# Products that nobody reads in four places, the first expert splits on ScalarE, one weight load and two read-outs moved

## What is computed

```python
x = L0_attn_resid_pre                                   # (2, 512, 256)
x = x + _L0_attn_ref(_layernorm(x), ...)   # 16 heads of 128, rotary, causal;
                                           # weights sgn*exp(|s| - max|s|), normed by their sum
x = x + _L0_ffn_ref(_layernorm(x), ...)    # routed in groups, top 4 of 16 experts
x = x + _L1_attn_ref(_layernorm(x), ...)   # 16 heads of 16, rotary, plain softmax
x = x + _L1_ffn_ref(_layernorm(x), ...)    # top 4 of 16 experts
# one expert: silu(x @ g.T) * (x @ u.T) @ d.T, times the token's weight, summed; a shared one without weight
```

## Time and profile before

| what | value |
|---|---|
| time, median of 3 runs | 890.24 us (885.75 to 897.82) |
| the profiled execution | 885.39 us, of which the span 883.7 us |
| PE, share of the span | 93% |
| DVE, ACT, POOL | 75%, 59%, 53% |
| mean granted TensorE clock | 0.984 |

### The profile page before, as it was taken

One profiled execution on the slowest core, in us unless ns is written; L12 is line 12 of the kernel. 1 busy time (PEld: TensorE's weight loads), 2 busy tenths in 40 slices (PEclk: granted clock), 3 DMA queues, 4 the chain that ended last, 5 costly groups with the idle time before them and its releaser, 6 DMA issues.

```text
span 883.7 us, 14685 instructions
## 1 busy us (share of the span) xinstructions
PE 825.5 (93%) x4500; PEld 625.8 (71%) x4500; DVE 659.3 (75%) x1354; ACT 519.3 (59%) x1099; POOL 468.9 (53%) x400
## 2 busy tenths in 40 slices
PE   4899999999999999878998999999999988999997
PEld 3678888778688888656787888654444446888886
DVE  5799999999988999788376865866777643576554
ACT  3688888778788888562544533354566564454442
POOL 3556666666456565533666776531300524566774
PEclk9999999999999999999999999978999999999999
DMA  4223222222332222112665458312431123334441
GB/s 141 104 96 97 96 95 95 96 96 86 127 96 96 95 95 96 48 67 73 206 221 180 137 156 281 116 57 75 130 132 50 55 74 114 117 122 139 149 155 66
DMA packets 57857, 99.97 MB, mean 113 GB/s; under 512 B 8320, under 2 KB 19072, under 8 KB 57792
## 3 DMA queue, kind: packets, MB, share of 16 engines
q1 hardware_dynamic: 57792, 99.17, 33.9%
HBM read 72.67 MB, written 9.57 MB: 93 GB/s over the span
## 4 chain that ended last, share of the span: by engine, by line
PE 64%; issue 12%; DVE 12%; POOL 9%; ACT 3%; DMA 1%; DVEq 0%; POOLq 0%; ACTq 0%; SPq 0%
PE ps L917 9%; PE ps L894 9%; PE ps L903 8%; PE ps L319 6%; PE ps L382 4%; PE ps L330 4%; PE ps L370 3%; POOL q_sin L515 3%; PE ps L1585 3%; PE ps L1555 3%; PE ps L343 3%; PE ps L1468 3%; PE ps L357 2%; PE ps L1489 2%; DVE nm L1779 2%
## 5 line engine op out<-in xcount | busy, mean ns | idle before, releaser
L1044 POOL TENSOR_TENSOR ew_lo<-ew_raw,ew_hi 128x768 fp32r<-128x768 f32 x68 | 127.7, 1879 | 69.3 <-ACT ew_hi L1009 41.3
L991 ACT ACTIVATE hid_hi<-guw 128x512 fp32r<-128x512 f32 x68 | 43.0, 632 | 160.2 <-POOL guw L1060 108.0
L1060 POOL TENSOR_TENSOR guw<-gu,cwb 128x512 f32<-128x512 f32 x64 | 84.7, 1324 | 98.2 <-issue 73.8
L1099 DVE TENSOR_TENSOR hid_lo<-guw,hid_hi 128x512 fp32r<-128x512 f32 x68 | 78.7, 1158 | 76.1 <-ACT hid_hi L991 76.0
L1779 DVE TENSOR_REDUCE nm<-ps 128x1 f32<-128x512 f32 x128 | 81.3, 684 | 24.7 <-PE ps L1489 24.5
L1674 ACT ACTIVATE e<-ps 128x512 f32<-128x512 f32 x128 | 69.0, 598 | 38.4 <-PE ps L1585 38.0
L502 DVE SCALAR_TENSOR_TENSOR w<-ex,rden,sgn 128x512 f32<-128x512 f32 (+3 forms) x128 | 90.9, 772 | 0.0
L430 ACT ACTIVATE ex<-sabs,nmax 128x512 f32<-128x512 f32 (+3 forms) x128 | 61.5, 552 | 43.1 <-DVE nmax L476 43.1
L515 POOL TENSOR_TENSOR q_sin<-q_sw,sin 128x512 f32<-128x512 f32 x64 | 85.0, 1348 | 1.4 <-DMA q_sw<-q_in 1.2
L917 PE MATMUL ps<-ew_hi,hid_hi 128*128 128x256 f32 x272 | 78.6, 289 | 5.9 <-DVE hid_lo L1099 4.4
L917 PE MATMUL ps<-ew_lo,hid_hi 128*128 128x256 f32 x272 | 77.2, 284 | 0.0
(11 more groups left out here) (181 smaller groups left out, 2403.9 us busy)
## 6 DMA issues: line engine op xcount, KB each, us to landing
ew_raw<-in_ew SPq DMA_DIRECT2D x68, 384.0 KB, 3.2
q_sw<-q_in SPq DMA_DIRECT2D x128, 128.0 KB, 2.0
cwb<-cw_dram SPq DMA_DIRECT2D x64, 256.0 KB, 3.7
wqk_raw<-in_wqk SPq DMA_DIRECT2D x32, 256.0 KB, 2.6
wv_raw<-in_wv SPq DMA_DIRECT2D x32, 128.0 KB, 2.6
wo_raw<-in_wo SPq DMA_DIRECT2D x32, 128.0 KB, 2.1
qs<-stk_q SPq DMA_DIRECT2D x16, 256.0 KB, 3.5
ks<-stk_k SPq DMA_DIRECT2D x16, 256.0 KB, 4.1
```

The source lines that it names most:

```text
L1044: pool.tensor_tensor(ff[f].ew[1][:, i % EW_SLOTS, :], ew_raw[:, i % RAW_SLOTS, :], fp(ff[f].ew[0][:, i % EW_SLOTS, :]), ALU.subtract).then ...
L1060: pool.tensor_tensor(ff[f].guw[:, i % 2, :], ff[f].gu[:, i % 2, :], ff[f].cwb[:, r % CWB_SLOTS, :], ALU.mult).then_inc(sem("guw"), 1)
L1099: dve.tensor_tensor(ff[f].hid[1][:, i % 2, :], ff[f].guw[:, i % 2, :], fp(ff[f].hid[0][:, i % 2, :]), ALU.subtract).then_inc(sem("hid_lo"), 1)
```

## The change

`warm` issues products on PE whose result no one reads: the bank that they write is overwritten by the next product there. It stands in four places: 14 at the start, as soon as the memset of `ones_r` on DVE is done, 10 more when the first `rstd` is made, 7 after the transposes of the output biases in step -2, and 2 ahead of each of the score tiles 26 to 31. The high parts of the expert items 0 to 4 are made on ACT at the end of the steps 27 to 31, ahead of what ACT did there; DVE made them in the steps 28 to 32. POOL's part of the norm and of the routing weights moves from step 27 to step 28. The load of item 8 moves behind the loads of the fourth and fifth `cwb` in both layers. In layer 1 the read-out of the last quad moves ahead of the activation of row 5, and its `normal` on DVE from row 6 to row 5.

```diff
@@ -613,7 +613,7 @@
                 pool.wait_ge(sem("xn"), NT)
                 pool.tensor_tensor(x[:, t:t + 2, :], x[:, t:t + 2, :],
                                    bo_row[:, 0, :].unsqueeze(1).broadcast_to([P, 2, D]), ALU.add).then_inc(sem("x_bo0"), 1)
-            if i == N0 - 5:
+            if i == N0 - 4:
                 ln_pool(pool, 1, (0,))
                 gw_low(pool, 0)
             if N0 - 4 <= i <= N0 - 1:
@@ -626,6 +626,11 @@
                 ew_low(pool, 0, 5)
                 weighted(pool, 0, 3)
 
+        def warm(pe, count, bank, src):
+
+            for _ in range(count):
+                pe.matmul(ps[:, bank, :], src[:, 0:P], src[:, 0:S], start=True, stop=True)
+
         def bias_rows(pe, k):
             for h in range(8 * k, 8 * k + 8):
                 last = pe.transpose(ps[:, BV_BANK[k] + h % 8 // 4, h % 4 * P:(h % 4 + 1) * P],
@@ -646,6 +651,7 @@
                         last = pe.transpose(ps[:, 7, k * D + c * P:k * D + (c + 1) * P],
                                             bo_in[:, k, c:c + 1].broadcast_to([P, P]), ident[:, :])
                 last.then_inc(sem("bo_ps"), 1)
+                warm(pe, 7, 3, ones_r)
             if i == N0 - 3:
                 pe.wait_ge(sem("q_rot"), 2 * N0)
                 ln_pe(pe, 1, (0,))
@@ -670,6 +676,8 @@
                 bias_rows(pe, 1)
 
         def a0_at_act(act, i):
+            if N0 - 5 <= i < N0:
+                ew_high_act(act, 0, i - (N0 - 5))
             if i == -3:
                 ln_act(act, 0, (0,))
                 act.wait_ge(sem("tab0"), 80)
@@ -710,22 +718,16 @@
                 ln_stats(dve, 1, 0)
             if i == N0 - 4:
                 ln_xn(dve, 1, 0)
-                ew_high_dve(dve, 0)
             if i == N0 - 3:
                 ln_low(dve, 1, 0)
-                ew_high_dve(dve, 1)
             if i == N0 - 2:
-                ew_high_dve(dve, 2)
                 gated(dve, 0, 0)
                 hid_low(dve, 0, 0)
                 routes[0] = ffn_route(dve, 0)
                 for part in range(3):
                     next(routes[0])
             if i == N0 - 1:
-                ew_high_dve(dve, 3)
                 next(routes[0])
-            if i == N0:
-                ew_high_dve(dve, 4)
             if i in (H0, N0):
                 h = i // H0 - 1
                 dve.wait_ge(sem("x_bo0"), 2 * h + 2)
@@ -755,7 +757,6 @@
         LAG3 = 9
         LOOP_AT = 4
         SPLIT_AHEAD = 2
-        FIRST_SPLITS = 5
         CWB_SLOTS = 3
         GU_BANKS = ((5, 6), (4, 7))
         GU_LATE = (2, 3)
@@ -836,7 +837,7 @@
             cw_store(0)
             for r in range(CWB_SLOTS):
                 cwb_load(r)
-            for i in range(2 * RAW_SLOTS, 3 * RAW_SLOTS):
+            for i in range(2 * RAW_SLOTS, 3 * RAW_SLOTS - 1):
                 ew_load(sp, f, i)
             for i, (m, h) in enumerate(ITEMS):
                 if i == CW1_AT[f]:
@@ -847,7 +848,7 @@
                     cwb_load(ROUTED[i] + 1)
                 if f == 0:
                     a1_row_sp(sp, i)
-                if LOOP_AT <= i and i + SPLIT_AHEAD + RAW_SLOTS < NI:
+                if LOOP_AT <= i + 1 and i + SPLIT_AHEAD + RAW_SLOTS < NI:
                     ew_load(sp, f, i + SPLIT_AHEAD + RAW_SLOTS)
 
         def logits(pe, f, h):
@@ -1000,15 +1001,13 @@
             wait_f(eng, f, f"ew_ld{i % RAW_SLOTS}", 16 * (i // RAW_SLOTS + 1))
             wait_f(eng, f, "y", i + 1 - EW_SLOTS)
 
-        def ew_high_dve(dve, i):
-            ew_high(dve, 0, i)
-            dve.tensor_copy(ff[0].ew[0][:, i % EW_SLOTS, :], ew_raw[:, i % RAW_SLOTS, :]).then_inc(sem("ew_hi_dve"), 1)
-
         def ew_high_act(act, f, i):
             ew_high(act, f, i)
             act.activation(ff[f].ew[0][:, i % EW_SLOTS, :], ew_raw[:, i % RAW_SLOTS, :], ACT.Copy).then_inc(sem("ew_hi_act"), 1)
 
         def row_act(act, f, i):
+            if (f, i) == (1, TAIL_ZT):
+                read_out(act, QUADS - 1)
             if i > LAG3:
                 hid_high(act, f, i - 1)
             silu_of(act, f, i)
@@ -1037,10 +1036,7 @@
                 a1_row_act(act, NI)
 
         def ew_low(pool, f, i):
-            if f == 0 and i < FIRST_SPLITS:
-                pool.wait_ge(sem("ew_hi_dve"), i + 1)
-            else:
-                pool.wait_ge(sem("ew_hi_act"), f * NI + i + 1 - FIRST_SPLITS)
+            pool.wait_ge(sem("ew_hi_act"), f * NI + i + 1)
             pool.tensor_tensor(ff[f].ew[1][:, i % EW_SLOTS, :], ew_raw[:, i % RAW_SLOTS, :], fp(ff[f].ew[0][:, i % EW_SLOTS, :]),
                                ALU.subtract).then_inc(sem("ew_lo"), 1)
 
@@ -1251,6 +1247,7 @@
         STEPS = QUADS * QT
         SLOTS = 6
         LEAD = 7
+        WARM_MAX = range(26, 32)
         LOW_DVE = 4
         S_BANKS = 3
         S_BANK = (3, 0, 1)
@@ -1486,6 +1483,8 @@
             if n % 8 == 0:
                 pe.wait_ge(sem(f"stage_ld{slot}"), 32 * ((2 * quad + j // 2) // SLOTS + 1))
             bank_wait(pe, "max", n)
+            if n in WARM_MAX:
+                warm(pe, 2, BANK_OF["max", n], xT_hi[:, 0, :])
             pe.matmul(ps[:, BANK_OF["max", n], :], qs[rows, slot, qi * P:(qi + 1) * P], ks[rows, slot, :],
                       start=True, stop=True).then_inc(sem("s1"), 1)
 
@@ -1660,8 +1659,6 @@
                 take(act, taken_at(ROW_LEAD[i], TAKEN_AT))
 
         def a1_tail_act(act, i):
-            if i == TAIL_ZT:
-                read_out(act, QUADS - 1)
             if i == TAIL_ZC:
                 chunk(act, B * DC - 1)
 
@@ -1822,7 +1819,7 @@
                     slot_dve(dve, ROW_LEAD[i], j)
 
         def a1_tail_dve(dve, i):
-            if i == TAIL_ZC:
+            if i == TAIL_ZT:
                 normal(dve, QUADS - 1)
             if i == TAIL_Y + 1:
                 ln_stats(dve, 3, 1)
@@ -1903,6 +1900,10 @@
 
         @block.tensor
         def _(pe):
+            pe.wait_ge(sem("ones"), 1)
+            warm(pe, 14, 7, ones_r)
+            pe.wait_ge(sem("ln_rstd"), 1)
+            warm(pe, 10, 7, ones_r)
             ln_pe(pe, 0, (0,))
             pe.wait_ge(sem("tab0"), 80)
             bias_rows(pe, 0)
```

## The result

The changed kernel takes 879.78 us (median of 6 runs, 878.49 to 881.78), the kernel before 890.35 (6 runs, 885.75 to 897.82). The ratio is 0.9885 [0.9852, 0.9918]: 1.2% faster, a little under half of the 2.4% forecast (10.6 us of 21.2), and within the 2% that I had set as "no change that can be told". In a later series, on another chip, the changed kernel took 885.12 and the one before 891.34, 0.9919 [0.9883, 0.9955]. 879.78 lies inside the range of 859 to 882, but not in the forecast's own 862 to 874; 885.12 lies outside both. (Medians and ranges of runs take in every run; ratios and their 95% intervals leave out the slow ones, which are over 1.5% above the fastest run of the same kernel.)

What follows compares the result with a forecast made beforehand. PE's own work was taken as the bound, holding 64% of the chain. Terms 3.3 + 7.0 + 2.0 + 3.4 + 3.4 = 19.1 off 885.4 gave 866.3; the median, 2.6 above, gave 869 us; range 859 to 882.

Steps and rivals of the forecast that it cites:

- the term of the last heads: Layer 0's last heads: moving high parts to ACT and POOL's norm part removes waits; 7.0 us gained, bounds 3.5 and 9.0.
- (a): Last heads: rstd no longer holds up POOL's split and sines; head 30's sines come 3.8 us earlier.
- (c): Last heads: head 31's masks no longer behind the second low part; DVE's 2.51 wait goes, running gain 7.5 us.
- (d): Last heads: ACT's copy of item 3 waits for its load, making ACT 3.0 late; running gain falls to 7.0 us.
- the second rival: Last heads: ACT's queue eats the gain via item 3's late load; 1 to 2 of 7.0 stay, 875 us; chance 0.12.
- the low parts stall: Expert rows: hid_lo takes 1.6 instead of 1.16 as POOL starts earlier against DVE; 34 us slower, 903; chance 0.04.
- PE is the bound all through: Whole kernel: POOL's and DVE's waits are cover, only the clock and 2 us stay; 879 us; chance 0.11.
- The start: Start and second head: added products give full clock for early transposes and remove a half clock; 3.3 us gained.
- The `cwb` loads: Expert rows: the fourth cwb loads earlier, so PE's wait before 429.75 goes; 2.0 us gained, bounds 1 and 2.0.
- The last read-out: Layer 1's end: PE's waits of 2.14 for zst and 1.48 for znT go; 3.4 us gained, bounds 1.5 and 3.6.
- The first maxima: Score tiles 26 to 31: twelve products lose 1.0, full clock returns 4.4; net 3.4 us gained.
- the rival of the clock: Steps 0 to 3: the clock falls anyway, 4.4 not gained and the twelve products cost up to 2; 875 us; chance 0.20.

Runs made afterwards that it cites:

- e4: Changed kernel with only 64 of 768 columns made in layer 0's low parts of items 0 to 4, the rest zeroed by memset: 883.01 us, ratio 0.9908.
- e10: e9 with ACT's copies of items 3 and 4 moved later, behind the first hid_hi and the silu of item 1: 876.71 us, ratio 0.9834.
- e9: Changed kernel with POOL making the low part of item 3 only behind cw and that of item 4 behind the second rstd: 880.56 us, ratio 0.9874.
- e2: Changed kernel with the high parts of items 0 to 4 back on DVE, POOL's norm part staying in step 28: 879.55 us, ratio 0.9886.
- r3: Repeat of e2 in a later series beside the changed kernel: 876.28 us, ratio 0.9823.
- e6: Changed kernel without the 31 products of the start and of step -2: 886.54 us, ratio 0.9959.
- e7: Changed kernel with the load of item 8 ahead of the fourth and fifth cwb again, in both layers: 886.15 us, ratio 0.9948.
- e5: Changed kernel without the twelve products ahead of score tiles 26 to 31: 885.05 us, ratio 0.9911.

## Why the prediction missed half of the gain

**The failed step is the term of the last heads**, "7.5 ... 7.0", of 19.1 in all. It measured -2.9, outside its bounds of 3.5 and 9.0, and failed twice.

First it was mis-sized. In (a) I added POOL's lateness, 3.8, and in (c) DVE's wait, as if PE would start earlier by all of it. PE had work between its two waits of 1.54 and 2.02, and gained these waits and no more: the lead goes from 0.8 at 358 to 4.5 at the norm's transposes, 3.7. That is my lower bound, "3.5, PE's two waits alone", and it did not even last: behind the next wait, for `v`, and the half clock at it, 1.5 of it is left at 397. The second trace gains 1.9 up to 397, the splits on DVE 2.4 and 2.3, and e4, with the low parts cut short, 3.1. So without any hold-up the term was worth 2 to 3.5 (the table's column "of it up to 419") and not 7.0. The check I gave, the transposes near 367, came out at 371.39. (The sum of the term doesn't close either: 7.5 less the 0.6 is 6.9, and 7.4 if the cast saved gives 0.5 back; I wrote 7.0.)

Second, it left out what gave it back, 6.6 from the transposes to 419, of which 4.4 lie behind 397: 2.5 are PE's longer wait for `z_lo`, and the rest falls with the half clock behind it. I asked which queue the copies were put into, ACT's, and (d) and the second rival went by that. ACT's stop was indeed 2.10 and PE's wait for it 1.05 longer, but that was made up by 397 (lead 2.4 behind 382, 2.3 there), and e10, which takes it away, gains no more than 0.2 over e9; its half clocks at 383.2 and 420.8, where e9 has none, blur this. I didn't ask where the copies would let POOL's low parts fall. With the copies on DVE POOL had to wait until DVE had cast, and then worked beside DVE's PSUM work and idle time. With the copies on ACT, made a step earlier, POOL runs its low part at once behind its own masks or `wo_lo`, which is just when DVE starts instructions that read SBUF only. e4 shows that POOL's length is what counts, e9 that its place is, and e2 and r3 that the copies on ACT caused it. What the half clocks near 376, 404 and 421 cost is in these numbers; that the one near 404 follows from the wait is shown by six traces against six. For the others it is only seen: after a wait of 2.33 for `v` the first trace has one, and e6 after 2.34 none.

I had the mechanism in hand as the rival "the low parts stall", with 0.04. I looked for it at `hid_lo` in the rows, priced it at 34 us and on the slow side, and never laid it over the one place where the change moves POOL against DVE. There it ate the gain. The rival named for that, ACT's queue, gave 875 and the wrong culprit. The range held in the first series because of its width. 879 was the number of the rival "PE is the bound all through", by chance: by that rival the waits of the last heads bring neither gain nor loss, but PE did gain 3.7 at the transposes and lost it again to DVE.

The other terms, by the leads and the runs with one part undone:

- *The start*, 3.3: 2.8 against the trace before, and 1.9 to 2.1 in the four traces with a half clock near 29. The 4.9 against e6 hold 2.1 of e6's own lateness. Right in kind, a little less in size: L319 first starts at 13.59, where 13.2 was forecast. That no half clock is left before 30 us is not sure: four of the eleven traces with these products have it, near 29.
- *The `cwb` loads*, 2.0: 1.4 (2.4 less 1.0), inside its bounds; PE's wait without them was 0.8 in this context and not 2.01, as in e7 PE came 4.4 later at 419 than in the trace before, and this `cwb` only 3.4 (429.95 against 426.60).
- *The last read-out*, 3.4: 3.5. Right, and right that the loads' order shows in layer 1 only with it.
- *The first maxima*, 3.4: 2.0. The net is smaller since DVE did not cover the products: they cost 3.9, more than my bound of 2.8, and not 1.0, as each tile's slot grew by 0.6 and DVE came to wait for it. What came back was 5.9, more than the 4.4 too; how much of it is the clock and how much slack that DVE left anyway no run separates. The clock stayed at 1.00 in every trace with the products and in none of the three without (two of the kernel before, e5). So the rival of the clock was wrong. The Trainium skill ("TensorE: Matmul & The Clock Gate", "Why this matters for your kernels"), by which there was no gap to fill, did not lead to what these rows show.

And one term was missing. In the heads, where nothing was changed, the first trace loses 2.0 against the one before, in two pieces of 1.0; the others lose 1.4 to 7.5 there (e4 9.5), in part in such pieces, in part at half clocks. DVE's timelines near 265 us, first of the changed kernel and then of the one before:

```profile
262.84 2.84 DVE L502 SCALAR_TENSOR_TENSOR w<-ex,rden,sgn 128x128 f32<-128x128 f32 x2
```

```profile
263.76 1.27 DVE L502 SCALAR_TENSOR_TENSOR w<-ex,rden,sgn 128x384 f32<-128x384 f32 x3
```

Two of the four `w` of this step are held beside POOL's `wqk_lo` and `q_sin`, and PE's transposes come 0.9 later. Of the 128 `w` of a trace 23 to 30 are over 0.5 longer than the shortest of their shape; which ones differs from run to run. The trace before has 27 itself, and its second trace, with 23, is 2.3 slower in the heads, so what a held `w` costs must depend on where it falls; that isn't shown further. Both profiles of the kernel before are near its fast end, so traces (5.3 apart) understate what the medians show (10.6 and 6.2).

## What to carry to other kernels

When a change lets one engine run earlier, lay its new place over what the engine that shares a port with it does at that moment; freeing POOL of a wait on DVE can cost DVE more than it gave POOL. Take as gain at most the waits of the bounding engine, not the lateness of those that feed it, and look for its next wait behind them: here 3.6 of waits gave 2. Where runs of one kernel spread by 1%, decide on small parts by the lead at each stage in two traces each, and then run the pick, since one median of four runs told none of these kernels from the changed one.

## What the runs showed of the hardware

A DVE instruction that reads two tensors in SBUF and starts while POOL's `ew_lo` runs gets next to nothing done until POOL is: begun at 372.82 beside a POOL instruction that ended at 374.20, it ended at 374.74, 0.5 later, and its own length is 0.69; 64 elements took 1.85 in place of 0.22. DVE's products with a PSUM operand beside POOL's sines (L465) kept their 0.7 each. It goes the other way too: the low part at 383.18 began beside DVE's 0.69 and took 2.33 in place of 1.83. The Trainium skill states this in "SBUF — State Buffer", "SBUF: two separate sides": whichever of the two starts first has the shared port pair for its whole instruction and the other is blocked. The traces agree, and I should have read them with it. It adds that DVE needs two SBUF inputs or a fast mode for it; `xn`, with one SBUF tensor, took 1.84 in place of 0.41 beside a low part in the kernel with the late low parts; in which mode it ran no row shows.

Six traces of PE standing 3.3 to 3.9 us and then at half clock, against six with 0.7 to 1.4 and at full, are the clearest case here of a DVE stall that PE pays twice: in the first trace 2.5 for the longer wait and 1.9 at the half clock. The stretch at 587 to 604 is the other kind: half clock with PE busy 16.4 of 16.9, cured by products that are themselves waste.
